# A graph kernel's edge loop: another order of four VectorE steps in each group of edges

## The reference

```
f    = (e @ fc_w.T).reshape(-1, 4, 128)              # e: 100000 x 128, fc_w: 512 x 128
w    = attn[rel]                                     # attn: 100 x 4 x 128
feat = sum over the 4 heads of leaky_relu(w * f, 0.2)
msg  = x[src] + feat
x    = layernorm(x + segment_sum(msg, dst))
```

## Time and profile before

| | us |
|---|---|
| median of 3 runs | 2623.32 (2622.6 to 2624.45) |
| span of the profiled execution, first to last instruction | 2618.1 |
| edge loop in it, first to last slope | 86.5 to 1485.8 |
| TensorE matmuls busy | 2159.8 (82%) |
| VectorE busy | 2255.1 (86%) |
| ScalarE busy | 1740.7 (66%) |
| GpSimd busy | 1919.3 (73%) |

### The profile page before, as it was taken

The page is one execution under the profiler, slowest core; times in us unless marked ns, Lnnn a source line. Parts: engine busy times, 40 slices in busy tenths (PEclk is TensorE's granted clock), DMA queues, the critical chain, the costliest instruction groups (busy, mean ns, idle before and its releaser), DMA issues.

```text
span 2618.1 us, 44445 instructions
## 1 busy us (share of the span) xinstructions
PE 2159.8 (82%) x11261; PEld 1538.3 (59%) x11261; DVE 2255.1 (86%) x5754; ACT 1740.7 (66%) x4973; POOL 1919.3 (73%) x1845
## 2 busy tenths in 40 slices
PE   6999999999999999999999846665666666666664
PEld 3566666666666666666666535565656565556554
DVE  9999999999999999999999976666666666677887
ACT  5888888888888888888888644444444444444446
POOL 2487777777777777777777647777777777777773
PEclk8999999999999999999999877777677767777776
DMA  4233333333333333333333233333333333333343
GB/s 133 78 100 104 104 104 103 106 103 102 103 103 105 104 105 105 103 103 102 103 104 104 65 95 81 80 80 80 81 81 80 81 81 82 79 81 79 80 80 80
DMA packets 156600, 244.04 MB, mean 93 GB/s; under 512 B 40836, under 2 KB 84398, under 8 KB 156226
## 3 DMA queue, kind: packets, MB, share of 16 engines
q1 hardware_dynamic: 97730, 132.55, 17.9%
q0 software_dynamic: 58624, 108.72, 17.5%
HBM read 231.99 MB, written 9.12 MB: 92 GB/s over the span
## 4 chain that ended last, share of the span: by engine, by line
DVE 36%; issue 25%; POOL 18%; PE 7%; DMA 6%; DVEq 5%; ACT 1%; POOLq 0%; SPq 0%; ACTq 0%
POOL room L583 17%; DVE y L1231 17%; DVE hs L1239 9%; DMA room<-h_rows,y 5%; DVEq L1211 4%; DVE room L1255 4%; PE FP L986 3%; DVE accT L1215 2%; PE FP L1007 2%; PE AP L1007 1%; DVE z L1224 1%; DMA room<-h_rows,idx 1%; DVE joh L1205 1%; POOL room L591 1%; DVE room L1247 1%
## 5 line engine op out<-in xcount | busy, mean ns | idle before, releaser
L539 POOL DMA_INDIRECT room<-in_x,pk x784 | 920.7, 1174 | 262.5 <-issue 251.0
L583 POOL DMA_INDIRECT room<-h_rows,y x756 | 714.7, 945 | 235.2 <-issue 216.0
L896 PE MATMUL FP<-fc_sb,room 128*128 128x512 f32 x1568 | 832.3, 612 | 2.2 <-issue 2.2
L905 PE MATMUL WP<-at_p,rel_oh 100*128 100x512 f32 x1568 | 803.5, 594 | 0.0
L986 PE MATMUL FP<-ident,room 128*128 128x128 f32 x1664 | 342.7, 370 | 385.9 <-DMA room<-h_rows,y 351.7
L659 ACT ACTIVATE w_sb<-WP 128x512 f32<-128x512 f32 x784 | 464.1, 592 | 225.0 <-PE WP L905 219.7
L986 PEld LDWEIGHTS FP<-ident,room 128*128 128x128 f32 x1664 | 291.0, 263 | 433.3 <-DMA room<-h_rows,y 387.1
L757 ACT ACTIVATE accT<-accT,neg_big 128x512 f32<-128x512 bf16 x208 | 150.0, 722 | 559.6 <-DVE accT L1377 559.6
L905 PEld LDWEIGHTS WP<-at_p,rel_oh 100*128 100x128 f32 x1568 | 297.8, 190 | 376.5 <-issue 376.5
L1224 DVE TENSOR_TENSOR z<-FP,w_sb 128x1024 f32<-128x1024 f32 x392 | 478.6, 1221 | 1.6 <-ACT w_sb L659 1.0
L1231 DVE SCALAR_TENSOR_TENSOR y<-z 128x2048 f32<-128x2048 f32 x196 | 452.4, 2308 | 0.0
(11 more groups left out here) (246 smaller groups left out, 3181.6 us busy)
## 6 DMA issues: line engine op xcount, KB each, us to landing
room<-in_e SPq DMA_DIRECT2D x196, 256.0 KB, 2.7
rel_sb<-in_rel_g SPq DMA_DIRECT2D x196, 200.0 KB
z<-sorted_sources SPq DMA_DIRECT2D x208, 128.0 KB, 3.0
room<-in_x,pk POOLq DMA_INDIRECT x784
room<-h_rows,y POOLq DMA_INDIRECT x756
sorted_edges<-runs,spot_i POOLq DMA_INDIRECT x196, 2.0
accT<-in_x_t SPq DMA_DIRECT2D x1, 3125.0 KB, 11.2
h_rows<-arena SPq DMA_DIRECT2D x13, 227.5 KB, 2.8
```

Source lines behind the costliest of these rows:

```text
L539: pool.indirect_dma_start(xg[:, k, u, 0:P], None, x[:, :], bass.IndirectOffsetOnAxis(ap=pk[:, g, u:u + 1], axis=0)).then_inc(xg_in[k], 16)
L583: pool.indirect_dma_start(hg[k][:, u, :], None, h_dram[:, :], bass.IndirectOffsetOnAxis(ap=sd[:, g * TG + u:g * TG + u + 1], axis=0)).then ...
L896: mm = pe.matmul(FP[u // 2][:, u % 2, :], e_sb[:, k, u, :], fc_sb[:, :], start=True, stop=True)
L905: mm = pe.matmul(WP[u % 2][:, :], rel_oh[:, k % 2, u * P:(u + 1) * P], at_p[:, j, :], start=(j == 0), stop=(j == 1))
```

## The change

In VectorE's `group`, `records` goes from ahead of the first `weigh_pair` to between `halve` and `finish`, and `add_x` goes ahead of `accumulate`. VectorE's order becomes: `z` (h = 0), `hs`, `joh`, `msg`, `z` (h = 1), x, accT, `y`. In the first group, which has no preceding one, `joh` follows the first `z`. No instruction is added or removed, and what each one waits for stays the same.

```
--- before.py
+++ after.py
@@ -1257,16 +1257,17 @@
 
             def group(g, k, lead):
                 prev = None if lead and k == 0 else (g - 1, (k - 1) % SLOTS, lead)
-                records(g, k, lead)
                 weigh_pair(g, k, lead, 0)
                 if prev:
                     halve(*prev)
+                records(g, k, lead)
+                if prev:
                     finish(*prev)
                 weigh_pair(g, k, lead, 1)
+                if prev:
+                    add_x(*prev)
                 if not (lead and k < 2):
                     accumulate(g - 2, (k - 2) % SLOTS, lead)
-                if prev:
-                    add_x(*prev)
                 slope(g, k, lead)
 
             with dve.Fori(0, pass_count(dve)) as p:
```

## The result

The changed kernel takes 2655.72 us (median of 4 runs, 2654.78 to 2657.36), the kernel before 2623.89 (4 runs): 1.012 times as long, 95% interval 1.0107 to 1.0133, 32 us slower. The span of the profiled execution is 2653.2 us, 35 more than before, and 33 of these lie in the edge loop: its first slope starts at 86.5 us as before and its last at 1519.0 instead of 1485.8, which is 7.346 us a group for 7.176. What follows the last slope takes 1134 us, before 1132.

A forecast was written before the change was run, and what follows sets the result against it. VectorE (994.7 of 1000 us busy) and TensorE's matmuls (999.7) were full. VectorE alone would need 7.27 us a group, a two-group loop through TensorE 7.38 for 7.18: 0.20 by 195 groups, +40, so 2663 us, range 2637 to 2675.

The forecast's parts named there:

- Nothing comes back at the slope: VectorE, slope to first `z`: stays 2.44 us without `joh`, since the wait for y_done holds `z` anyway; gain 0.
- 0.09 lost before `msg`: VectorE, `hs` to `msg`: `joh` puts 0.20 us of work into a 0.11 hole, so 1.25 becomes 1.34.
- The swap is neutral: VectorE, second `z` to slope: x and accT trade places, same three gaps, 1.73 us either way; register load hidden.
- The loop over two groups: Late `joh` delays TensorE's compaction, then ScalarE's fourth copy and the next second `z`: 14.76 us for two groups, 7.38 each.
- copy to `z`: Wait from the end of ScalarE's fourth copy to VectorE's second `z`, costed at 0.13 us.
- what TensorE regains: TensorE, compaction to next group's fourth copy: shortened when sums no longer wait for x; 0.03 us taken, between 0 and 0.24.
- The weight loads' row: TensorE judged by its weight loads' busy share, 619.9 us of 1000: 38% to spare, so it would catch up.
- the first rival: TensorE catches up on the late compaction: period 7.28 us, +0.09 to 0.10 a group, 2642 us; chance 0.22.
- GpSimd at 0: GpSimd's DMAs add 0 us: the one slowed at the slope (1.85 for 0.94) gets that back in a longer period.
- near 0.25 us of idle matmuls: Sign in the profile after: TensorE's compaction waits for `joh` in most groups, its matmuls idle near 0.25 us in each.
- The faster rival: `z` directly follows the slope without `joh`, and the hole before `msg` is filled: 2600 to 2617 us; chance 0.05.
- the one without change: Slope to `z` shrinks by 0.10, paying for the 0.09; buffers cover the late compaction: 2622 us; chance 0.06.

The follow-up runs named there:

- the third experiment: Kernel before, with the one-hot moved between the first product and the first halving: 2666.0 us, ratio 1.0161.
- the fourth experiment: Changed kernel, with the compaction on TensorE and ScalarE moved behind the next group's first product and its copy: 2634.43 us, ratio 1.004.
- the run where TensorE bounds (period 7.11): Kernel before with accT between the halvings and, from the fifth group on, one x-row gather a group left out: 2611.22 us, ratio 0.9961.

## Why the prediction was right

The forecast was 2663 us, the measurement is 2656: the direction, the cause and the shape were right, the size 40 us for 32. By its steps:

- **Nothing comes back at the slope.** Right: 0.13 from the slope's end to `z` before, after and with the one-hot elsewhere. That the one-hot was covered at its old place is shown by the third experiment.
- **0.09 lost before `msg`.** Right: `hs` to `msg` went from 1.25 to 1.34. VectorE's own sum rose by less, 0.057, mainly because the slope takes 2.28 for 2.31 us in the new order.
- **The swap is neutral.** Right, within 0.1%.
- **The loop over two groups.** Right, shown by the alternating periods and by the fourth experiment, which removes it. Term by term from the rows above, 804.02 to 818.70: `joh` 0.28; to the compaction 0.06 (costed 0.05); to the end of the next group's fourth copy, 812.19, 7.83 (7.85); copy to `z` 0.08 (0.13); `z` to slope 1.74 (1.73); slope to `z` 2.42 (2.44); `z` to `hs` 1.14 (1.14); `hs` to `joh` 1.13 (1.14). The sum is 14.68, costed 14.76.
- **The size** was off in three terms of this sum: copy to `z`, for which I had put the 0.13 of the slope's wait (0.05 less), the slope's length (0.02 less), and what TensorE regains (0.02 more).
- **TensorE's room.** The term came out at 7.83, so TensorE regained 0.05 of the 7.88 before; I had put 0.03. In the run where TensorE bounds (period 7.11) the same stretch takes 7.82, so 0.05 or 0.06 was all the room there was. But my reason for a small number was not sound, and that it came so near is partly luck: the row of the matmuls, from which I took it, doesn't show room. It reads 1000.0 us busy of 1000 at a period of 7.11, 999.7 at 7.18 and 999.8 at 7.23 with the same matmuls in each group, and still 994.7 at 7.40. "Full" in that row isn't "can't go faster"; the length of the stretch in a run that TensorE bounds is what shows it.
- **The weight loads' row.** The rule of the Trainium skill, "Perfetto Trace Analysis", section "Identifying the Most-Contended Engine", would have given the first rival, 2642. The trace goes against it here: with the weight loads busy 619.9 us of 1000 TensorE had 0.06 us of room in a group, not 0.24.
- **The rule of the Trainium skill that a semaphore costs nothing extra** ("VectorE: DVE Perf Modes", section "The DRAIN you can't avoid") would have left VectorE's sum as it was. It rose by 0.057 in the fourth experiment, where VectorE bounds alone.
- **GpSimd at 0** held for this change, since it lengthens the period. The reason given, that it "gets that back", was wrong: the held DMA took 2.00 in the changed kernel for 1.85, and GpSimd stayed without a pause, but no engine waited for it. In the other direction the same row was worth over 200 us.

Among the signs it named, "near 0.25 us of idle matmuls" a group was too much: it is 0.16. The faster rival and the one without change fell with the 0.13 behind the slope.

## What to carry to other kernels

Before a step is moved into a hole, ask what its old place costs: if it lies inside another wait, it is free there, and moving it only adds. Then ask who reads its result: a reader on another full engine turns lateness into a loop, whose length in groups (here two) gives the price, the sum of its terms divided by that number. And before a bound is lowered, hold the next engine's period against it; an engine at 79% busy can be full when its idle time is all of fixed gaps, and one at 100% in a row whose ends are modelled can still have a little room.

## What was not expected

- GpSimd's indirect DMAs are held when they start while VectorE's slope runs: one that normally takes 0.94 us takes 1.85 when it starts 1.28 behind the slope's start, and 3.02 when it starts 0.12 behind. Both end 3.1 us after the slope's start, 0.8 after its end. One that is already under way isn't held: the DMA at 804.15 in the earlier trace rows, 0.01 ahead of the slope, takes 0.98. The first halving, `hs`, holds them in the same way. It hardly shows in the earlier trace rows, where the DMA at 808.84 starts 0.13 before the end of `hs` and would end 0.8 after it anyway, but it does in the kernel before with one gather left out, where the DMA ends 0.8 after the end of `hs`:

```profile
803.17 1.22 DVE L1239 TENSOR_TENSOR hs<-y 128x1024 f32<-128x1024 f32 x1
803.25 1.95 POOL L539 DMA_INDIRECT room<-in_x,pk  x1 [0.30 <-issue]
```

The products `z`, which read `FP` from TensorE's sums, don't do that: the DMA behind it starts at 805.50, 0.48 into a `z`, and takes 0.94. With five DMAs a group this makes a step: at a period of 7.17 GpSimd keeps up, and at 7.11 it loses its place and the mean period becomes 8.3.
- The length of the slope, the same instruction on the same data, depends on the order around it: medians in the steady stretch are 2284 ns in the changed kernel, 2307 before, 2336 with the one-hot before the halving. That is up to 10 us over the loop; what causes it stays open.
